# Folded keys, values and bias made once in the first walk and loaded a batch ahead

## The reference, cut to what matters

```
x = x + xattn(layernorm(x), ctx)          # 16 heads of 64, keys and values from ctx, biases bq bk bv bo
x = x + dense(layernorm(x)) + sparse(layernorm(x))
xattn:  q = xn Wq + bq;  k = ctx Wk + bk;  v = ctx Wv + bv
        softmax(q k^T / 8) v, then Wo, + bo
dense:  causal attention, 16 heads of 16, then a gated FFN of 1024, with two rms norms
sparse: top 2 of 8 experts of 256, rms norm
```

## Time and profile before

| | |
|---|---|
| Runs | 1475.77 us median of 3 (1472.37 to 1482.32) |
| Profiled execution, its own time | 1476.62 us |
| Its span | 1474.9 us, mean granted TensorE clock 0.974 |
| Busy | TensorE 1361.7 us (92%), VectorE 808.0, GpSimd 600.6, ScalarE 575.0 |
| DMA | 115.39 MB, mean 78 GB/s |
| First walk, from its first `m` | 22.7 to 154.5 us |
| Merged walk of batch 2, from its first `m` | 299.2 to 439.7 us |

### The profile page before, as it was taken

How to read it: one execution, slowest core, us unless ns; L and a number is a source line. 1 busy time by engine, 2 the same in 40 slices (tenths; PEclk the granted TensorE clock), 3 DMA queues, 4 the chain that set the end, 5 groups by cost and what they waited for, 6 DMA issues and landing times. The chain is left out here.

```text
span 1474.9 us, 22385 instructions
## 1 busy us (share of the span) xinstructions
PE 1361.7 (92%) x7229; PEld 885.5 (60%) x7230; DVE 808.0 (55%) x1654; ACT 575.0 (39%) x1214; POOL 600.6 (41%) x1051
## 2 busy tenths in 40 slices
PE   6887999999999989998999999999999889999995
PEld 6543556656665667566656665666566346666674
DVE  2626645754585368445753675376547623333348
ACT  2231553055316421651265125514540544444446
POOL 4312343253326342533254334423532445555544
PEclk9998899999999999999999999999999899999997
DMA  6054205110501050105000500140032534422245
GB/s 215 1 164 136 73 1 132 41 30 1 153 19 30 5 161 10 29 21 147 20 16 29 144 17 15 52 121 17 1 98 62 168 105 129 129 87 87 86 188 191
DMA packets 78297, 115.39 MB, mean 78 GB/s; under 512 B 24840, under 2 KB 66208, under 8 KB 75648
## 3 DMA queue, kind: packets, MB, share of 16 engines
q1 hardware_dynamic: 67888, 79.69, 18.1%
q10 hardware_dynamic: 3840, 16.78, 4.3%
q0 software_dynamic: 6480, 17.77, 3.4%
...
## 5 line engine op out<-in xcount | busy, mean ns | idle before, releaser
L1540 DVE TENSOR_REDUCE nm<-ps 128x2 f32<-128x256 f32 (+3 forms) x256 | 200.2, 818 | 75.8 <-PE ps L970 73.8
L1229 ACT ACTIVATE room<-ps 128x512 f32<-128x512 f32 x320 | 179.9, 599 | 152.1 <-PE ps L996 151.9
L1051 PE MATMUL ps<-hT,w 128*128 128x512 f32 x768 | 206.6, 412 | 0.0
L703 POOL TENSOR_SCALAR_AFFINE_SELECT room<-room 128x256 f32<-128x256 f32 (+1 forms) x320 | 121.3, 390 | 137.7 <-ACT room L1229 133.2
L1051 PEld LDWEIGHTS ps<-hT,w 128*128 128x128 f32 x768 | 140.8, 191 | 33.6 <-DVE hT L1570 2.0
L969 PE MATMUL ps<-room 96*128 96x128 bf16 (+3 forms) x512 | 126.5, 315 | 37.0 <-DMA room<-parts_d 18.0
L1253 ACT ACTIVATE room<-ps 128x512 f32<-128x512 f32 x64 | 37.2, 593 | 270.1 <-PE ps L1051 270.1
L1087 PE MATMUL ps<-room 128*128 x284 | 135.4, 599 | 1.9 <-ACT room L1281 1.9
L1061 PE MATMUL ps<-w,room 128*128 128x256 f32 x512 | 129.3, 391 | 7.6 <-DVE room L1591 7.6
L920 PE MATMUL ps<-room 128*128 128x256 f32 x512 | 123.1, 384 | 2.8 <-ACT room L1190 1.8
L901 PE MATMUL ps<-room,xnT 128*128 128x512 f32 x256 | 122.0, 601 | 0.0
...
## 6 DMA issues: line engine op xcount, KB each, us to landing
...
```

The source lines that it names most:

```text
L703: done(g.affine_select(out=w, in_=w, compare_op=ALU.is_ge, fill=0.0, base=0, pattern=[[0, 2]] * (blocks - 1) + [[1, P]], channel_multiplie ...
L1051: last = mm(bank(up_banks(b, m)[i]), w[:, x, k, m * P:(m + 1) * P], hT[:, y, k, :], start=((x, y, k) == terms[0]), stop=((x, y, k) == term ...
L1229: done(fn(prob[:, u * 512:(u + 1) * 512], bank(score_bank(b) + n % 2), ACT.Exp), "b_exp")
L1540: done(v.tensor_reduce(nm[:, t, 2 * hp:2 * hp + 2], pair_ps, AX.X, ALU.max, negate=True), "a_max")
```

## The change

M, bqk and VW of batches 1 to 7 are no longer made in each batch's walk from loaded keys and values. The first walk makes all of them, stores them to DRAM (`m_d`, `vw_d`, `bqk_d`), and SP loads a batch's set (2.6 MB) during the maxima of the batch before.

In the first walk `kp` (8 steps) makes the keys of a pair of heads for all batches, `kf` (16) multiplies them with Wq: 64 rows of the pair's one head into bank 4 and the 64 rows of the other into bank 5, 448 columns each (7 batches of 64); with every second `kf` one product of 448 columns adds the pair's part of bqk in bank 7. ScalarE drains bank 4, VectorE bank 5. `m_out` stores two pairs (two DMAs of 0.9 MB, ScalarE's queue). These 27 steps stand between the cross attention steps of batch 0. `vp` (8) and `vf` (16; four products of 64 rows and 256 columns, both banks drained by ScalarE) and `vw_out` (8 stores of 1.0 MB) stand among `v`, `route`, `slots` and the maxima up to the eighteenth. The staging buffers lie in the room of w1 and w3, which are not loaded until later.

In merged walks `m`, `bqk`, `vw`, their copies and GpSimd's `bq_bc` are gone. `CROSS` begins with both `x_turn`, `cs 0 0`, `shift 1`, `cs 0 1`, `f_hb`, `exp 0`, `sum 0`, `x_bias`; the 55 score steps are spread over 21 places from `cs 0 1` on. Batch 0's own folds and its list (`CROSS_FIRST`) stay as they were. SP waits for the replicated rows to have landed before it loads the next set, and in the first walk for all stores.

The diff, cut to its core:

```diff
+CROSS = [("x_turn", 0), ("x_turn", 1), ("cs", 0, 0), ("shift", 1), ("cs", 0, 1), ("f_hb",), ("exp", 0), ("sum", 0), ("x_bias",)]
+CROSS += CROSS_FIRST[CROSS_FIRST.index(("cs", 1, 0)):]
...
-    first, last = CROSS.index(("bqk", 0)), CROSS.index(("ct", 3, 1))
+    first, last = CROSS.index(("cs", 0, 1)), CROSS.index(("ct", 3, 1))
     slots = [i for i, s in enumerate(CROSS) if s[0] in ON_PE and first <= i <= last]
...
+K_FOLDS = [s for p in range(PAIRS) for s in [("kp", p), ("kf", p, 0)] + ([("m_out", p // 2 - 1)] if p % 2 == 0 and p else []) + [("kf", p, 1)]]
+V_FOLDS = [s for p in range(PAIRS) for s in [("vp", p), ("vf", p, 0)] + ([("vw_out", p - 1)] if p else []) + [("vf", p, 1)]]
+V_FOLDS = [("vp", 0), ("m_out", PAIRS // 2 - 1)] + V_FOLDS[1:] + [("vw_out", PAIRS - 1)]
...
+    cross = [s for s in CROSS_FIRST if not of_previous(s)]
+    tail = [s for s in TAIL if not of_previous(s)]
...
+    for i, s in enumerate(cross):
...
+        if i in slots:
+            want = (slots.index(i) + 1) * len(K_FOLDS) // len(slots)
+            order += K_FOLDS[given:want]
+            given = want
+    given = 0
+    for s in tail:
+        order.append(s)
+        at_max = s[0] == "max" and s[2] % 2 == 1
+        want = given + (3 if s[0] in ("route", "slots") else 1 if s[0] == "v" else 2 if at_max else 0)
+        order += V_FOLDS[given:want]
+        given = min(want, len(V_FOLDS))
+    assert given == len(V_FOLDS), given
...
-        m_sb = part(0, 2048).rearrange("p (k n) -> p k n", k=KD)
-        vw = part(2048, 2048).rearrange("p (a n) -> p a n", a=PAIRS)
-        bqk = part(4096, 1024)
+        m_first = part(0, 2048).rearrange("p (k n) -> p k n", k=KD)
+        vw_first = part(2048, 2048).rearrange("p (a n) -> p a n", a=PAIRS)
+        bqk_first = part(4096, 1024)
+        vw_next = part(5120, 2048).rearrange("p (a n) -> p a n", a=PAIRS)
+        m_next = part(7168, 2048).rearrange("p (k n) -> p k n", k=KD)
+        bqk_next = part(9216, 1024)
...
+        m_stage = [s[:, 0:KD * (B - 1) * 4 * CK].rearrange("p (k b n) -> p k b n", k=KD, b=B - 1) for s in stage]
+        vw_stage = [s[:, i * 2048:(i + 1) * 2048].rearrange("p (c n) -> p c n", c=B // 2) for s in stage for i in range(2)]
...
-        kt_d = internal("kt_d", (PAIRS, P, B * CK))
-        vt_d = internal("vt_d", (PAIRS, P, B * CK))
+        m_d = internal("m_d", (B, P, KD, CH * CK))
+        vw_d = internal("vw_d", (B // 2, 2, CK, CH, D))
+        bqk_d = internal("bqk_d", (B, CH, CK))
...
-            def load_kv(b):
-                before(sp, b, "vw_ps")
-                for dst, src in ((k_bd, kt_d), (v_bd, vt_d)):
-                    for i in range(2):
-                        half = slice(i * CHD, (i + 1) * CHD)
-                        done(sp.dma_start(dst[half, :, i * CK:(i + 1) * CK],
-                                          src.rearrange("a p n -> p a n")[half, :, span(b, CK)]), "kv_in", 16)
+            def load_kv(n):
+                need(sp, n - 1, "sc_ps", T)
+                need(sp, n - 1, "sc_add", T)
+                need(sp, n - 1, "pv_ps", T)
+                done(sp.dma_start(m_next, m_d[n, :, :, :]), "kv_in", 16)
+                done(sp.dma_start(bqk_next, bqk_d[n, :, :].rearrange("h k -> (h k)").partition_broadcast(P)), "kv_in", 16)
+                for j in range(2):
+                    done(sp.dma_start(vw_next[j * CK:(j + 1) * CK, :, :],
+                                      vw_d[n // 2, n % 2, :, :, :].rearrange("k (a j) m -> k a j m", j=2)[:, :, j, :]), "kv_in", 16)
 
...
+                    if c is not None and b != B - 1:
+                        need(sp, b, "rep_q", per["rep_q"])
+                        need(sp, b, "rep_k", per["rep_k"])
+                        sp.sem_inc(freed, 1)
+                        load_kv(b + 1)
                     send_shifts(b, 0)
                     if c is None:
+                        for i in range(2):
+                            sp.wait_ge(m_out[i], 16 * KD * PAIRS // 4)
+                        sp.wait_ge(p0["bqk_out"], 16)
                         for i in range(4):
-                            sp.wait_ge(kv_out[i], 16 * 2 * PAIRS // 4)
+                            sp.wait_ge(kv_out[i], 16 * PAIRS // 4)
                         sp.sem_inc(freed, 1)
                         load_kv(b + 1)
...
+                    if kind in ("kp", "vp"):
+                        i = step[1] + (PAIRS if kind == "vp" else 0)
+                        if i >= 1:
+                            pe.wait_ge(p0["kv_sb"], i)
                         else:
                             pe.wait_ge(sems["kv_in"], 64)
-                        w = (wk_c, wv_c)[i % 2]
+                        w = wk_c if kind == "kp" else wv_c
                         for k in range(KD):
-                            last = mm(bank(6 + i % 2), w[:, k, (i // 2) * P:(i // 2 + 1) * P], ctxT[:, k, :], start=(k == 0), stop=(k == KD - 1))
+                            last = mm(bank(6), w[:, k, step[1] * P:(step[1] + 1) * P], ctxT[:, k, :], start=(k == 0), stop=(k == KD - 1))
...
+                    elif kind == "kf":
+                        pa, k = step[1:]
+                        if k == 0:
+                            pe.wait_ge(p0["kv_sb"], pa + 1)
+                        f = 2 * pa + k
+                        if f:
+                            pe.wait_ge(p0["fold_act"], f)
+                            pe.wait_ge(p0["fold_dve"], f)
+                        keys = kv_st[pa % 2]
+                        if k:
+                            if pa == 0:
+                                pe.wait_ge(p0["ident"], 13)
+                            mm(bank(7, (B - 1) * CK)[0:CH, :], bqx[:, pa * CH:(pa + 1) * CH], keys[:, CK:], start=(pa == 0), stop=(pa == PAIRS - 1), skip_group_check=True)
+                        for j in range(2):
+                            rows = slice(j * CHD, (j + 1) * CHD)
+                            last = mm(bank(4 + j, (B - 1) * CK), wqT[rows, pa, k * P:(k + 1) * P], keys[rows, CK:], start=True, stop=True)
+                        last.then_inc(p0["fold_ps"], 1)
+                    elif kind == "vf":
+                        pa, half = step[1:]
+                        if half == 0:
+                            pe.wait_ge(p0["kv_sb"], PAIRS + pa + 1)
+                        f = 2 * pa + half
+                        pe.wait_ge(p0["fold_act"], 2 * PAIRS + f + (1 if f else 0))
+                        if f == 0:
+                            pe.wait_ge(p0["fold_dve"], 2 * PAIRS)
+                        values = kv_st[2 + pa % 2]
+                        for two in range(2):
+                            for j in range(2):
+                                rows = slice(j * CHD, (j + 1) * CHD)
+                                at = (half * 2 + two) * 2 * CK
+                                last = mm(bank(4 + j, D, two * D), values[rows, at:at + 2 * CK], wo_c[rows, pa, :], start=True, stop=True)
+                        last.then_inc(p0["fold_ps"], 1)
                     elif kind == "x_turn":
-                        turn(b, xh, (0, 1), lambda t2: [("xn1", 1), (("m_act", "m_dve")[t2], 1)], "xT1", step[1:])
+                        if c is not None:
+                            need(pe, c, "a_max", per["a_max"] - 1 + step[1])
+                        turn(b, xh, (0, 1), lambda t2: [("xn1", 1)] + ([(("m_act", "m_dve")[t2], 1)] if c is None else []), "xT1", step[1:])
...
+                    if kind == "kp":
                         i = step[1]
...
-                            fn(kv_st[i % 4], bank(6 + i % 2), ACT.Identity, bias=bk[:, i // 2:i // 2 + 1], scale=CHD ** -0.5).then_inc(p0["kv_sb"], 1)
-                        else:
-                            fn(kv_st[i % 4], bank(6 + i % 2), ACT.Identity, bias=bv[:, i // 2:i // 2 + 1]).then_inc(p0["kv_sb"], 1)
-                        act.wait_ge(p0["kv_sb"], i + 1)
-                        act.dma_start((kt_d, vt_d)[i % 2][i // 2, :, :], kv_st[i % 4]).then_inc(kv_out[i % 4], 16)
+                        act.wait_ge(p0["kv_ps"], 4 + i + 1)
+                        if i >= 2:
+                            act.wait_ge(p0["fold_ps"], 2 * (i - 1))
+                        fn(kv_st[i % 2], bank(6), ACT.Identity, bias=bk[:, i:i + 1], scale=CHD ** -0.5).then_inc(p0["kv_sb"], 1)
...
+                        pa, k = step[1:]
+                        duo = pa // 2
+                        act.wait_ge(p0["fold_ps"], 2 * pa + k + 1)
+                        if duo >= 2:
+                            act.wait_ge(m_out[duo % 2], 16 * KD)
+                        fn(m_stage[duo % 2][:, k, :, pa % 2 * P:pa % 2 * P + CK], bank(4, (B - 1) * CK).rearrange("p (b n) -> p b n", n=CK), ACT.Copy).then_inc(p0["fold_act"], 1)
+                        if pa == PAIRS - 1 and k:
+                            fn(kv_st[0][0:CH, 0:(B - 1) * CK], bank(7, (B - 1) * CK)[0:CH, :], ACT.Copy).then_inc(p0["fold_act"], 1)
+                            act.wait_ge(p0["fold_act"], 2 * PAIRS + 1)
```

(42 more changed lines are left out.)

137 lines of the change are left out of this document (62 added, 75 removed).

## The result

The changed kernel took 1544.8 us (median of 4 runs, 1540.5 to 1552.2) beside 1474.5 us for the kernel before (median of 4). The ratio is 1.047, 95% interval 1.042 to 1.053: slower, by 70 us where 44 were forecast. The time lies inside the forecast range, near its upper end. The profiled execution of the changed kernel spans 1538.8 us against 1474.9, at a mean granted clock of 0.966 against 0.974.

What follows compares the result with a forecast made beforehand. The prediction took TensorE's instruction stream, its work plus its waits, as the bound. Its terms 33 + 3 + 8.9 + 6 - 6.6 gave +44 us on the profiled execution's 1476.6: forecast 1520, range 1486 to 1548.

Steps and rivals of the forecast that it cites:

- the sign: Whole kernel: slower by more than 1%, chance 0.75; faster by more, 0.07.
- the first walk: Batch 0 up to batch 1's start: cross attention +33 us, routing stage +3, maxima +8.9, start of batch 1 +6.
- which waits: Merged walks: TensorE idle before the second score step, unit 4 and the first `va`, 1 to 2.5 us each.
- the merged walks' term: Batches 2 to 7: 1.1 us won per batch, -6.6 us in all.
- Added waits in the same walks: Walks of batches 1 to 7: 8.25 us of new TensorE waits per batch, against 9.3 us of work removed.
- the first `va`: Merged walk: waits 2.55 us for the cuts, as GpSimd's 2.4 us bias add stands ahead of them.
- no further wait: Merged walk after the first `va`: VectorE has 15 us of work left in some 45, so no more waits.
- (a): First walk's folds: row halves run in turn, `kf` 1.5 and `vf` 1.7 us, total 1538; chance 0.20.
- (b): Merged walks: half of the waits absent, 4.5 us won per batch, total 1484; chance 0.20.
- (c): Merged walks: only the x turns' 1.5 us wait stays, seven batches win 7.8 each, first walk +25, total 1446; chance 0.07.
- (d): First walk: `kf` and `vf` from pair 4 on wait for stores, +15 us, total 1550; chance 0.08.
- (e): Folded loads miss their batch, needing over 40 us for 2.6 MB; chance 1 in 100, counted in (d).

Runs made afterwards that it cites:

- experiment 4: Changed kernel with both 64-row halves of every key and value fold on rows 0 to 63 (result wrong, same work): 1573.0 us.
- experiment 5: Changed kernel with w1 and w3 loaded before the second set of shifts in the first walk and split three maxima before its end: 1540.4 us.
- 1, order: Changed kernel with exp 0, sum 0 and x_bias placed later in merged walks and score units dealt unevenly over the first seven slots: 1521.6 us.
- 2, bias add: Changed kernel with only x_bias moved, behind the first turns of the probabilities (ct 0) instead of ahead of cs 1: 1523.0 us.
- 6, value folds spread: On top of experiment 5, value folds spread over the first 26 maxima and the next pair's projection put ahead of the pair's folds: 1530.7 us.
- 7, early turns: Changed kernel with the next batch's x turned between a walk's last two maxima, in banks 4 and 5: 1533.3 us.
- 8, all: Changed kernel with the reordering, early w1 and w3 loads, spread value folds and early x turns together: 1500.8 us.
- 9, keys ahead: On top of "8, all", batch 1's folded keys and bias loaded once stored, ahead of w1, w3 and the values, with their own semaphore: 1492.6 us.
- 10, one product: On top of "9, keys ahead", the first tile's product with reciprocal sums in merged walks made on VectorE instead of GpSimd: 1469.9 us.
- 11, four products: As "10, one product", but the product with reciprocal sums is on VectorE for all four tiles of a merged walk: 1466.7 us.
- 12, before with the edit: Control: the kernel before, with the product with reciprocal sums moved from GpSimd to VectorE for all four tiles in merged walks: 1474.8 us.
- experiment 3: Changed kernel with the four loads of folded keys, bias and values made twice for every batch: 1560.8 us.

## Why the prediction was right and where not

**Right: the sign, the first walk.** Key folds take 0.95 us (0.9 forecast) and value folds 1.07 (1.0), side by side (experiment 4). The end of cross attention, at the first turn behind it, moved by 34.1 us (76.2 to 110.3; +33). A group of four maxima with folds takes 6.93 us (161.00 - 154.07 in the timeline; 6.8), the first sixteen maxima 27.5 (27.2). From the end of the maxima to batch 1's first `cs` the kernel takes 1.9 us more (2.1), and that start is set by the loads of w1 and w3 behind the folded loads, as walked out; experiment 5 takes the wait away. The stretch from the first `v` to the maxima was mis-sized: 33.5 us where 28.3 were, +5.2 and not +3. Two stretches that the forecast left alone were shorter, by 2.4 us (the turns and q/k ahead of `v`) and 1.2 (the last maxima). That the sum comes to 46.8 against 47 is in part luck.

**Right: which waits.** The places of the merged walk, their order and their releasers, in the walk of batch 6 all of them.

**Wrong: the merged walks' term.** From batch 1's first `cs` to batch 7's the forecast was -6.6 and the profiled executions have +12.6 (854.9 to 867.5). These 19.2 us are nearly all that the forecast of +44 lacks against the measured 63.9. The step that failed is "Added waits in the same walks": I priced each wait at its own length and took TensorE's clock behind it for unchanged. In these six stretches the records of the granted clock have 38.9 us at half speed in the changed kernel and 13.7 in the kernel before. Half of the 25.2 between them is 12.6 us; with it taken off, the six are as long as before, where 1.1 us each were to be won. So by this estimate 12.6 of the 19.2 us are the clock and 6.6 are waits that I had too short, unit 4's and the first `va`'s among them (2.50 and 3.15 in the walk of batch 6, for 2.05 and 2.55).

All executions say the same more broadly. The time lost to the clock is at most (1 - mean granted clock) × span, as if TensorE were never idle at half clock. Means over the executions:

| kernel | executions | granted clock | lost at most, us | span less that, us |
|---|---|---|---|---|
| before (run beside the experiments) | 40 | 0.976 | 35 | 1439 |
| changed | 4 | 0.961 | 60 | 1484 |
| 1, order | 4 | 0.963 | 56 | 1464 |
| 2, bias add | 5 | 0.968 | 49 | 1473 |
| 5, early w1 and w3 | 4 | 0.961 | 60 | 1477 |
| 6, value folds spread | 4 | 0.967 | 50 | 1479 |
| 7, early turns | 4 | 0.962 | 58 | 1474 |
| 8, all | 6 | 0.972 | 41 | 1457 |
| 9, keys ahead | 4 | 0.975 | 37 | 1452 |
| 10, one product | 8 | 0.983 | 25 | 1443 |
| 11, four products | 6 | 0.982 | 26 | 1439 |
| 12, before with the edit | 12 | 0.976 | 35 | 1439 |

By this estimate the change costs at least 45 us in work and waits, where the forecast had 44 (the profiled pair alone gives 50), and up to 25 more by the clock, which the forecast left out. The same columns place gains that the waits leave open. In experiment 2, 11 us are waits and up to 11 the clock; in 10, 9 and up to 12; in 6, all of it is the clock. And the 10 us by which experiment 11 is ahead of the kernel before are clock as well: in work and waits the merged walks win what the first walk pays.

That the clock hangs on the waits is argued, not shown wait by wait. In the six stretches half-clock time goes 38.9, 32.6, 30.6, 19.9 and 13.0 us in the changed kernel and in experiments 8 to 11. But the walks of experiments 3 to 6 have the changed kernel's order and 42.7 to 54.7 us, experiments 1 and 7 have 41.8 and 48.6 with fewer waits, and batch 6's walk keeps its clock at the wait of unit 4, where the walks of batches 3, 4, 5 and 7 lose it.

**Also mis-sized: the first `va`** (2.55 forecast; 1.12 where the clock had fallen ahead of it, 3.15 where it had not), and the later `va` waits that I took for none ("no further wait"). GpSimd holds up `va` 28 times in seven walks, for 24.4 us in all.

**The rivals.** (a), halves in turn, is refuted. (b), a looser chain, was not so. Its price had a slip: half of the 8.25 us absent wins 5.2 a batch, not 4.5, which gives 1480. (c) was right in its logic, though no run of the change itself shows it: with unit 4's wait at 0.47 and the waits of `va` halved, a walk wins 5.9 us (experiment 11), the first walk costs 26.5 where (c) had 25, and 3.6 was given as the point from which the sign turns. (d), stores piling up, shows only as waits of a few us (L920 behind ScalarE). Its price was off too: 15 us on the sum give 1535, not 1550. (e) didn't happen; experiment 3 doubles the loads, and the merged walks hardly notice.

**Still open**: whether a given wait makes the clock fall; and whether VectorE's subtraction is slower because GpSimd works beside it.
